# Hybrid attention and mixture kernel: shift rows straight from SBUF to SBUF, eleven quads of lead instead of twelve, and another table of side work

## What is computed

```python
x = x + attn_a(layernorm(x))     # differential attention, 16 heads, two sub-heads of 4 features each
x = x + ffn(layernorm(x))        # 64 experts, top 8, one shared expert
x = x + attn_b(layernorm(x))     # softmax over a 16 x 16 energy per batch
x = x + ffn(layernorm(x))

# attn_a: q, k, v = split(x @ w_qkv.T); per sub-head
p = softmax(q @ k.T * scale); a = p @ v          # 1024 x 1024 scores, 32 sub-heads, 2 batches
o = rms_norm(a1 - lam * a2) * (1 - LAMBDA_INIT); return o @ w_proj.T + b_proj

# attn_b: energy[a, b] = sum over tokens of q[a] * k[b]; softmax; mixes v; @ Wo + bo

# ffn
aff = xf @ centroids.T; idx = top_k(aff + expert_biases, 8)
w = sigmoid(aff[idx]); w = w / sum(w); cw = scatter of w into 64 columns
h = silu(xf @ W_up[e]); y = (h @ W_down[e]); out = shared + sum over e of cw[e] * y
```

## Time and profile before

| | |
|---|---|
| median of 3 runs | 1092.47 us (1088.93, 1092.47, 1094.38) |
| the profiled execution | 1090.65 us, of which the span 1088.8 us |
| TensorE busy | 1001.9 us (92%), granted clock 0.979 on average |
| VectorE busy | 959.6 us (88%) |
| ScalarE busy | 890.0 us (82%) |
| GpSimd busy | 485.9 us (45%) |
| preparation, until the first maximum | 0 to 36.6 us |
| attention a | 36.6 to about 656 us |
| feed-forward parts and attention b | about 656 to 1088.8 us |

### The profile page before, as it was taken

How to read it: one execution, slowest core, us unless ns; L and a number is a source line. 1 busy time by engine, 2 the same in 40 slices (tenths; PEclk the granted TensorE clock), 3 DMA queues, 4 the chain that set the end, 5 groups by cost and what they waited for, 6 DMA issues and landing times.

```text
span 1088.8 us, 21671 instructions
## 1 busy us (share of the span) xinstructions
PE 1001.9 (92%) x8016; PEld 515.6 (47%) x8016; DVE 959.6 (88%) x1186; ACT 890.0 (82%) x1466; POOL 485.9 (45%) x893
## 2 busy tenths in 40 slices
PE   6389999999999999999999999999899999999998
PEld 3022222222222222222222236787677777777876
DVE  7799999999999999999999947798866988787665
ACT  5179999999999999999999987777775787678765
POOL 3363555455555544564556467342413431323331
PEclk9579999999999999999999999999999999999999
DMA  8911110111011101100110008575757466757763
GB/s 277 304 30 50 52 51 4 50 51 51 4 51 51 37 17 51 51 26 28 52 51 22 3 8 192 144 187 131 173 150 179 136 160 179 194 145 182 197 190 90
DMA packets 80473, 108.91 MB, mean 100 GB/s; under 512 B 23536, under 2 KB 33520, under 8 KB 80368
## 3 DMA queue, kind: packets, MB, share of 16 engines
q1 hardware_dynamic: 66336, 100.98, 34.4%
q10 hardware_dynamic: 14032, 6.55, 2.3%
HBM read 95.57 MB, written 11.93 MB: 99 GB/s over the span
## 4 chain that ended last, share of the span: by engine, by line
DVE 54%; PE 27%; ACT 7%; issue 6%; DMA 5%; POOL 1%; SPq 1%; ACTq 0%; DVEq 0%; POOLq 0%
DVE NEGMAX L1065 46%; PE PS L1456 7%; PE PS L1458 7%; PE PS L1457 7%; PE PS L1358 2%; DVE HF L1106 2%; DVE HL L1114 2%; ACT PR L858 2%; DMA GATE<-gate_d 1%; PE PS L1331 1%; ACT PS L955 1%; ACT HH L948 1%; ACT L955 1%; DVE ln_st L1000 1%; DMA shift_d<-SHT 1%
## 5 line engine op out<-in xcount | busy, mean ns | idle before, releaser
L1065 DVE TENSOR_REDUCE NEGMAX<-PS 128x1 f32<-128x1024 f32 x512 | 584.6, 1208 | 10.4 <-PE PS L1294 9.7
L858 ACT ACTIVATE PR<-PS 128x512 f32<-128x512 f32 x1024 | 538.9, 600 | 37.1 <-PE PS L1331 24.2
L1358 PE MATMUL PS<-PR,VG 128*32 128x256 f32 (+1 forms) x3840 | 321.3, 406 | 17.3 <-ACT PR L858 2.0
L1331 PE MATMUL PS<-QB,KB 32*128 32x512 bf16 x1024 | 260.1, 387 | 3.7 <-DMA QB<-shift_d 2.5
L1294 PE MATMUL PS<-KA,QA 32*128 32x512 bf16 x1024 | 204.3, 397 | 31.2 <-DVE NEGMAX L1065 22.4
L1106 DVE TENSOR_TENSOR HF<-PS,GATE 128x1024 f32<-128x1024 f32 x128 | 156.2, 1221 | 72.7 <-ACT PS L955 62.3
L1331 PEld LDWEIGHTS PS<-QB,KB 32*128 32x128 bf16 x1024 | 75.0, 91 | 239.8 <-ACT PR L858 137.4
L955 ACT ACTIVATE PS<-PS 128x1024 f32<-128x1024 f32 x128 | 129.2, 1010 | 71.5 <-PE PS L1458 70.9
L948 ACT ACTIVATE HH<-HF 128x1024 fp32r<-128x1024 f32 (+1 forms) x136 | 139.8, 1029 | 34.4 <-DVE HF L1106 32.6
L770 POOL TENSOR_TENSOR HL<-HF,HH 128x1024 fp32r<-128x1024 f32 (+1 forms) x32 | 69.2, 2162 | 165.8 <-ACT HH L948 165.8
L1358 PEld LDWEIGHTS PS<-PR,VG 128*32 128x32 f32 x3840 | 76.4, 108 | 130.7 <-issue 64.6
(11 more groups left out here) (186 smaller groups left out, 970.1 us busy)
## 6 DMA issues: line engine op xcount, KB each, us to landing
GATE<-gate_d SPq DMA_DIRECT2D x256, 256.0 KB, 4.1
QA<-q_stack SPq DMA_DIRECT2D x64, 128.0 KB, 2.6
QB<-q_stack SPq DMA_DIRECT2D x16, 256.0 KB, 2.9
KB<-k_stack SPq DMA_DIRECT2D x16, 256.0 KB, 3.0
KA<-k_stack SPq DMA_DIRECT2D x60, 64.0 KB, 2.4
q_stack<-PARTS SPq DMA_DIRECT2D x12, 256.0 KB, 4.4
k_stack<-PARTS SPq DMA_DIRECT2D x12, 256.0 KB, 4.6
RAWU<-in_L_ffn_W_up_dram ACTq DMA_DIRECT2D x4, 512.0 KB, 13.0
```

What stands on the lines that cost most here:

```text
L858: nc.scalar.activation(PR[:, s % PRING, r, :], PS[:, SCORE_BANK[n], :], ACT.Exp, scale=SCALE_A).then_inc(p_ready, 1)
L1065: nc.vector.tensor_reduce(NEGMAX[:, hs % 2, col:col + 1], PS[:, e:e + 2, :].rearrange("p b n -> p (b n)"), axis=AX_X, op=ALU.max, negate=T ...
L1331: mm(PS[:, SCORE_BANK[n], :], KB[strip, u, mt * P:(mt + 1) * P], QB[strip, u, half * BANK:(half + 1) * BANK], start=True, stop=True).then_ ...
L1358: last = mm(PS[STRIP * r:STRIP * (r + 1), 7, cols], VG[:, u, mt, r // 2, :], PR[:, s % PRING, r, cols], start=mt == 0, stop=mt == TB - 1 a ...
```

## The change

- The strips' rows are laid out by feature, then slot (4 features x 8 slots) instead of slot, then feature. Slot 6 holds zeros, slot 7 (rows 7, 15, 23, 31 of a strip) takes the three shift parts and a fourth row of zeros. One DMA writes all slots of a part, so a batch takes 8 DMAs instead of 14.
- The shift goes from `SHT` to `QB` in one DMA; `shift_d` is gone. GpSimd's four operations write another order of columns, and there is one more memset ahead of the first.
- LEAD is 11. The shift is transposed in quad 6 (before: 5), between the first half of the weighted values and the third score matmul (before: after the fourth), and copied ahead of quad 6's maxima (before: between those of quad 5).
- `SIDE`: the tail's entries move with LEAD; `gate_T` of chunks 1, 2, 4 and 6 goes from (n, 15) to (n, 16); the routing of chunk 3 starts one to three steps earlier with `gate_T` as before; the gram chain starts a step earlier and `x_T` of attention b goes behind it. GpSimd does the last `heads_norm` after the side work of (0, 4), whose root it was ahead of.

```diff
-STACK_WRITES = 16 * 2 * (len(Q_SLOTS) + 1)
+STACK_WRITES = 16 * 2 * 4
-LEAD = 12
+LEAD = 11
...
 def shift_at(g):
-    return (g + 3) // TB if (g + 3) % TB == 0 and 0 <= (g + 3) // TB < 2 * NG else None
+    return (g + 2) // TB if (g + 2) % TB == 0 and 0 <= (g + 2) // TB < 2 * NG else None
...
-        if shift_at(g) is not None:
-            tiles["shift", shift_at(g)] = len(tiles)
+            if p == 1 and shift_at(g) is not None:
+                tiles["shift", shift_at(g)] = len(tiles)
...
-    NQ - 8: [("x_T", ("f", 0))], NQ - 7: [("affinity", 0)], NQ - 6: [("top", 0)], NQ - 5: [("sum", 0)], NQ - 3: [("gate_T", 0)],
+    NQ - 7: [("x_T", ("f", 0))], NQ - 6: [("affinity", 0)], NQ - 5: [("top", 0)], NQ - 4: [("sum", 0)], NQ - 2: [("gate_T", 0)],
...
-    (0, 14): [("heads", 1)], (0, 15): [("gate_T", 1)],
+    (0, 14): [("heads", 1)], (0, 16): [("gate_T", 1)],
...
-    (1, 13): [("sum", 2)], (1, 14): [("norm", ("f", 3))], (1, 15): [("gate_T", 2)],
-    (2, 1): [("x_T", ("f", 3))], (2, 4): [("affinity", 3)], (2, 6): [("top", 3)], (2, 7): [("sum", 3)], (2, 8): [("gate_T", 3)],
+    (1, 13): [("sum", 2)], (1, 14): [("norm", ("f", 3))], (1, 16): [("gate_T", 2)],
+    (2, 0): [("x_T", ("f", 3))], (2, 1): [("affinity", 3)], (2, 3): [("top", 3)], (2, 4): [("sum", 3)], (2, 8): [("gate_T", 3)],
...
-    also((n, 9), ("x_T", ("b", c)))
-    also((n, 10), ("gram", b))
-    also((n, 11), ("gram_k", b))
-    also((n, 12), ("q_k", b))
-    also((n, 13), ("energy", b))
-    also((n, 14), ("soft_exp", b), ("soft_mix", b))
+    also((n, 9), ("gram", b))
+    also((n, 10), ("gram_k", b))
+    also((n, 11), ("q_k", b))
+    also((n, 12), ("energy", b))
+    also((n, 13), ("soft_exp", b), ("x_T", ("b", c)), ("soft_mix", b))
...
-    also((n + 1, 15), ("gate_T", f))
+    also((n + 1, 16), ("gate_T", f))
...
             def write_parts(b, part):
...
                     places = [c for c, a in enumerate(slots) if a == part]
-                    for c in places:
-                        rows = stack[b * GPB:(b + 1) * GPB, :, HD_A * c:HD_A * (c + 1), :].rearrange("g r d n -> (g r) d n")
-                        sp.dma_start(rows, src).then_inc(st_w[b], 16)
+                    step = places[1] - places[0] if len(places) > 1 else 1
+                    rows = stack[b * GPB:(b + 1) * GPB].rearrange("g r d c n -> (g r d) c n")[:, places[0]:places[-1] + 1:step, :]
+                    sp.dma_start(rows, src.unsqueeze(1).to_broadcast([P, len(places), SEQ])).then_inc(st_w[b], 16)
...
             def shift_rows(s, half):
...
+                if half == 0:
+                    sp.wait_ge(sh_w, 16 * (s + 1))
                 sp.wait_ge(sht_ok, hs + 1)
-                sp.dma_start(shift_d[half].rearrange("a r (t n) -> (a r t) n", n=P), SHT[:, half, :]).then_inc(sh_w, 16)
-
-                sp.wait_ge(sh_w, 48 * s + 16 * (half + 2))
-                for r in range(R):
-                    lo = STRIP * r + SHIFT_ROW
-                    sp.dma_start(QB[lo:lo + 3, u, half * BANK:(half + 1) * BANK], shift_d[half, :, r, :]).then_inc(sh_r, 16)
+                sp.dma_start(QB[SHIFT_SLOT:P:SLOTS, u, half * BANK:(half + 1) * BANK], SHT[:, half, :]).then_inc(sh_r, 16)
...
             for k in (2 * NG - 2, 2 * NG - 1):
                 output(k)
-                heads_norm(k)
+                if k < 2 * NG - 1:
+                    heads_norm(k)
...
                 side((n, w))
+                if (n, w) == (0, 4):
+                    heads_norm(2 * NG - 1)
...
             def max_quad(s):
 
+                if shift_at(s) is not None:
+                    shift_out(shift_at(s))
                 for key in quad_items(s):
...
-                    if key[2] == 0 and shift_at(s) is not None:
-                        shift_out(shift_at(s))
-                if not quad_items(s) and shift_at(s) is not None:
-                    shift_out(shift_at(s))
...
-                    dve.wait_ge(sh_w, 48 * (hs // 2 - 1) + 16 * (hs % 2 + 2))
-                nc.vector.tensor_copy(SHT[:, hs % 2, :], PS[0:3 * SHIFTS, SCORE_BANK[n], 0:P // 2].bitcast(BF16)).then_inc(sht_ok, 1)
+                    dve.wait_ge(sh_r, 16 * (hs - 1))
+                nc.vector.tensor_copy(SHT[:, hs % 2, :], PS[0:4 * SHIFTS, SCORE_BANK[n], 0:P // 2].bitcast(BF16)).then_inc(sht_ok, 1)
...
                     weighted_values(s - 1, 0)
+                if shift_at(s) is not None:
+                    shift_tile(shift_at(s))
                 if scored:
                     scores(s, 2)
                 m_items(items[1:2])
                 if scored:
                     scores(s, 3)
-                if shift_at(s) is not None:
-                    shift_tile(shift_at(s))
...
                     elif stage == "gram":
+                        pe.wait_ge(ln_xn, LN["b", 2 * arg + 1] + 1)
```

More of the change, by code:

```diff
@@ L40 @@
 K_SLOTS = (2, 1, 0, 0, 0, 1)
-SHIFT_ROW = HD_A * len(Q_SLOTS)
 STRIP = 32
-STACK_WRITES = 16 * 2 * (len(Q_SLOTS) + 1)
+SLOTS = STRIP // HD_A
+SHIFT_SLOT = SLOTS - 1
+STACK_WRITES = 16 * 2 * 4
 MAX_LOADS = 16 * 2 * R
@@ L365, in hybrid_layer @@
         OTS = sb("OTS", [P, 2, BANK], where=attn)
-        SHP = sb("SHP", [P, 2, 3 * SHIFTS], BF16, where=attn)
-        SHT = sb("SHT", [3 * SHIFTS, 2, P], BF16, where=attn)
+        SHP = sb("SHP", [P, 2, R, 4, SHIFTS // R], BF16, where=attn)
+        SHT = sb("SHT", [4 * SHIFTS, 2, P], BF16, where=attn)
         ZERO = sb("ZERO", [P, SHIFTS], where=attn)
@@ L470, in fill_shift_rows @@
                 for stack, fill in ((q_stack, ZEROS), (k_stack, ONES)):
-                    rows = stack[b * GPB:(b + 1) * GPB, :, SHIFT_ROW:STRIP, :].rearrange("g r s n -> (g r) (s n)")
-                    sp.dma_start(rows, fill[:].unsqueeze(1).to_broadcast([P, 2, SEQ])).then_inc(st_w[b], 16)
+                    rows = stack[b * GPB:(b + 1) * GPB].rearrange("g r d c n -> (g r d) c n")[:, len(Q_SLOTS):SLOTS, :]
+                    sp.dma_start(rows, fill[:].unsqueeze(1).to_broadcast([P, SLOTS - len(Q_SLOTS), SEQ])).then_inc(st_w[b], 16)
             def write_parts(b, part):
@@ L498, in load_strips @@
             def load_strips(stack, tile, u, g, there):
-                sp.dma_start(tile[:, u, :], stack[g].rearrange("r s n -> (r s) n")).then_inc(there, 16)
+                sp.dma_start(tile[:, u, :], stack[g].rearrange("r d c n -> (r d c) n")).then_inc(there, 16)
             def load_max(u, g, keys=True):
@@ L640, in shift_parts @@
                 pool.wait_ge(m_free, ITEM["max", TB * hs + TB - 1, 1] + 1)
-                u, w = hs % 2, SHIFTS
-                nc.gpsimd.tensor_tensor(SHP[:, u, 0:w], NEGMAX[:, u, :], ZERO[:], op=ALU.add).then_inc(sh_split, 1)
+                u = hs % 2
+                top, rest = (t.rearrange("p (r t) -> p r t", r=R) for t in (NEGMAX[:, u, :], SHR[:]))
+                nc.gpsimd.tensor_tensor(SHP[:, u, :, 0, :], top, ZERO[:].rearrange("p (r t) -> p r t", r=R), op=ALU.add).then_inc(sh_split, 1)
                 pool.wait_ge(sh_split, (4 * hs + 1))
-                nc.gpsimd.tensor_tensor(SHR[:], NEGMAX[:, u, :], SHP[:, u, 0:w], op=ALU.subtract).then_inc(sh_split, 1)
+                nc.gpsimd.tensor_tensor(rest, top, SHP[:, u, :, 0, :], op=ALU.subtract).then_inc(sh_split, 1)
                 pool.wait_ge(sh_split, (4 * hs + 2))
-                nc.gpsimd.tensor_tensor(SHP[:, u, w:2 * w], SHR[:], ZERO[:], op=ALU.add).then_inc(sh_split, 1)
+                nc.gpsimd.tensor_tensor(SHP[:, u, :, 1, :], rest, ZERO[:].rearrange("p (r t) -> p r t", r=R), op=ALU.add).then_inc(sh_split, 1)
                 pool.wait_ge(sh_split, (4 * hs + 3))
-                nc.gpsimd.tensor_tensor(SHP[:, u, 2 * w:3 * w], SHR[:], SHP[:, u, w:2 * w], op=ALU.subtract).then_inc(sh_split, 1)
+                nc.gpsimd.tensor_tensor(SHP[:, u, :, 2, :], rest, SHP[:, u, :, 1, :], op=ALU.subtract).then_inc(sh_split, 1)
                 pool.wait_ge(sh_split, (4 * hs + 4))
@@ L658, in _ @@
             link(nc.gpsimd.memset(ZERO[:], 0.0))
+            link(nc.gpsimd.memset(SHP[:], 0.0))
             shift_parts(0)
@@ L774, in _ @@
                 side(where)
-                if where == NQ - 11:
+                if where == NQ - 10:
                     heads_norm(2 * NG - 3)
```

18 lines of the change are left out of this document (9 added, 9 removed).

## The result

Over seven executions the changed kernel took 1115.89 us in the median (1114.69 to 1124.05), the kernel before 1090.13 (1088.74 to 1094.38, seven executions): the ratio is 1.0237, interval 1.0209 to 1.0264. It is slower by 25.8 us. Forecast were 1103 and a range of 1079 to 1110: the side is right, the sum of the terms (+12.7) is half of what came, and the time lies outside the range.

What follows compares the result with a forecast made beforehand. Bound: VectorE's row maxima in attention, TensorE in the feed-forward part. Terms 12.3 - 1.9 - 2.1 + 12.8 - 5.5 - 2.4 - 0.5 = +12.7 on 1090.65 gave 1103 us, range 1079 to 1110.

Steps and rivals of the forecast that it cites:

- The copy waits for the transposition: Attention: VectorE's shift copy ahead of quad 6's maxima waits 0.41 us in each of 30 halves, +12.3 us.
- Late shifts: Attention: one shift DMA instead of five ends the places where scores wait for late shifts, -1.9 us.
- No scores that wait for shifts: Sign expected in the chain of the profile after: attention scores no longer wait for shifts to land.
- Gates a pair later: Feed-forward chunks 1, 2, 4 and 6: later gates make the whole stage 3.2 us later each, +12.8 us.
- rival E: Feed-forward: the forecast 1103 plus TensorE clock dips of 1.5 us at three chunks, 1107.5 us; chance 0.06.
- The start of the scores: Preparation and first scores: no cost forecast; fewer stack writes taken as 0, and the lead priced only at the tail.
- Chunk 3's routing: Feed-forward: routing moved earlier removes the gate transposition's 4.00 us wait and 1.5 of half clock, -5.5 us.
- Eleven steps of lead: Attention tail: one quad less is left once the maxima are done, -2.1 us, bounds 0 and -2.3.
- Root first: Feed-forward start: root taken before the last heads' norm, norm wait 2.42 becomes 1.5 without clock dip, -2.4 us.
- Gram chain: Feed-forward: chain a pair earlier removes part of 0.50 us waits before the mix's transposition at two places, -0.5 us.

Runs made afterwards that it cites:

- second profile: The changed kernel, unedited, run once more for another profile: that profiled execution took 1115.17 us; median 1116.72, ratio 1.0242 to the kernel before.
- gates at 15: Changed kernel with the gate transposition of chunks 1, 2, 4 and 6 back from step 16 to 15: 1101.57 us, ratio 1.0089 to the kernel before.
- the copy between the maxima: Changed kernel with VectorE's shift copy after quad 6's first maximum instead of ahead of it: 1104.51 us, ratio 1.0111 to the kernel before.
- three edits: Changed kernel with gates at 15, the shift copy between quad 6's maxima and 14 writes per batch: 1084.55 us, ratio 0.9943 to the kernel before.
- the old table: Changed kernel with all of `SIDE` as before (tail entries moved for the lead) and the last heads' norm ahead of the root: 1106.53 us, ratio 1.0133.
- The two large edits undone together: Changed kernel with gates at 15 and the shift copy between quad 6's maxima, eight writes kept: 1086.34 us, ratio 0.9956 to the kernel before.

## Why the prediction was right and wrong

- **The copy waits for the transposition: right.** Forecast 0.41 a half and 12.3; the profile shows 18.74 for 18.32, 30 x 0.42 = 12.6, and undoing it gave 11.4. VectorE recovered nothing, and TensorE was no earlier.
- **Late shifts: right** for all but the first. 1.9 forecast; 0.35 us of irregular halves are left of 1.85. "No scores that wait for shifts" fails at the first scores, below.
- **Gates a pair later: right in mechanism, a little low.** 12.8 forecast, 14.3 measured, 11.5 in the kernel before; 12.4 in the four chunks of the profiles. Part of it is the clock, which the term left out and rival E had with a chance of 0.06. In the second profile it fell at three of the four places, as E said, in or behind waits of 3.32 (TensorE for the sum at 791), 3.44 and 3.82 us:

```profile
790.00:795.00 5.00, 3.61 (x11) 2.92 (x12) 4.90 (x18) 3.32 (x4) 0.73 (x1) 0.50 0.42 117
900.00:905.00 5.00, 2.75 (x10) 2.30 (x11) 4.61 (x7) 3.51 (x4) 0.61 (x1) 0.77 1.07 232
1015.00:1020.00 5.00, 4.28 (x15) 3.49 (x16) 4.62 (x4) 3.61 (x5) 0.57 (x1) 0.66 0.98 227
```

  These levels lie between 1.2 and 2.4 GHz as means of 5 us at either. With gates at 15 the last two places show 1.00; the first still shows 0.75 from 785 to 790, behind the wait of 1.79. The 1.5 us a place of rival E were too much where it can be compared: with the copy between the maxima TensorE waited 3.43 at chunk 4's gates and the clock stayed full, and chunks 3 and 4 together took 113.8 us, against 114.3 in the second profile with its dip. The prediction had the new waits in pieces of 1 to 2.5 us; at three places they were one longer piece, at chunk 1's gates 0.92 and 1.47. The rule of the Trainium skill cited there held at these three places: the matmuls behind the wait ran at the half clock. It needs a wait that lets the clock fall, and the 3.43 didn't.
- **The start of the scores, costed at 0: the first step that failed.** For the writes the text had "I take **0**, because the first shift split later waits for the second batch's writes", and for the lead "The number of maxima stays; one quad less is left once they are done", with no price at the start. It priced one load and not the order behind it. Measured: the second copy 4.8 us later in its distance from the first, of which 0.4 is the copy's own wait. Between the two copies VectorE waited 0.88 us before and 5.1 in both profiles. Shown is that ScalarE's copy of the up weights, ahead of its first exponential, holds the first scores and with them the maxima: 2.4 of the 4.8 go when it goes. RAWU's four loads land later beside the larger writes (18.3 to 19.2 us in the median of a profile's four in the ten profiles with eight writes a batch, 10.7 to 15.8 in the nine with 14, the kernels with the old layout among them), but 14 writes alone brought no gain that shows. For the other 2.4 the rows show where VectorE waits, behind the first shift's DMA and behind matmuls at half the clock. That LEAD and the later transposition are the cause (one quad less of cover, one quad more of scores before the copy) was argued from the order and not tried.
- **Chunk 3's routing, -5.5: the second.** The 4.00 us went, but "Its gate transposition keeps its place (2, 8), so the 4.00 goes" left out what the moved stages put in ScalarE's queue: 2.4 of 5.2 came back at the end of chunk 1. Net -2.8 in the profiles, -4.3 in the medians. Nor did the half clock leave this place: it came behind the new wait of 1.79 (mean 0.66 from 770 to 775 with three edits).
- **Eleven steps of lead, -2.1: right for the tail**, 2.2, but its own bound, "0, if the gates end last there", holds in part: with the old table chunk 0 is 1.4 longer (62.3 against 60.9), the products of chunk 0 waiting 3.1 us for its gates (1.0 before).
- **Root first: right in the profiles**, 2.42 became 1.49 and the chunk 2.4 shorter; the medians show 1.3. **Gram chain, -0.5:** nothing measurable.

Sum for the second profile: 12.6 (copy) - 1.5 (late shifts) - 0.4 (the first maximum comes that much earlier) + 4.4 (start of the scores) + 13.7 (gates, 439.8 - 426.1) - 2.2 and + 1.4 (lead) - 2.8 (routing) - 2.4 (root) = 22.8 of 24.6. The 1.8 left isn't settled; RT's wait, 0 to 3.0 us per place and execution, is of that size. The two large edits undone together give 29.6 in the medians where singly they give 25.7. By the ratios to the kernel before on the same chip the two figures are 30.7 and 29.9, so the runs don't show that the edits help each other.

The range failed because the side terms had no bound on the costly side: routing (taken at its best bound), root, gram, lead and writes could only gain or be 0, and neither the work of a moved stage nor the start of the scores had a cost in it.

## What to carry to other kernels

A step moved one place on a path of fixed length (transposition, copy, DMA out, DMA in, product) cost its whole shift here where the end of the path had nothing to spare (12.4 us in four chunks), though it removed 5.6 us of waits; idle time in front of it was cover, not loss. Where the engines waited for something else anyway, at the gates of chunks 5 and 7, it cost nothing. So look at the path's end first. Where a stage is moved ahead, read the queue of every engine on which it has work, and count the table loads on ScalarE. When lead is taken off, look at the one-time work ahead of the first step on each engine: here it was ScalarE's copy of 3.6 us that showed, though the lead's own share was not tried alone.
